# A gated attention, WKV and mixture-of-experts stack: late expert weights in raw buffers of their own, and the hand-written order of work behind the last attention tile

## The chip, the cores and the metric

The kernel runs on one core of one Trainium2 chip. Its time is the device time of one launch in microseconds; a median of several launches is given. Below, PE is TensorE, DVE is VectorE, ACT is ScalarE, POOL is GpSimd and SP is SyncE.

## What is computed

The input x has 16 batches of 64 tokens of 256 values. Four residual blocks follow one another, each on a LayerNorm of x and with a tanh gate:

```python
x = x + tanh(g_xattn[0]) * attention(layernorm(x), mask, ctx)      # 32 heads of 8, rope, additive mask, plus an adapter over ctx
x = x + tanh(g_ffn[0]) * moe0(layernorm(x))                        # 8 experts of 256x256, the best one, its softmax weight
x = x + tanh(g_xattn[1]) * wkv(w, u, layernorm(x), ctx)            # running max, exp, decayed sums over the 64 tokens
x = x + tanh(g_ffn[1]) * moe1(layernorm(x))                        # 8 experts, top 2, integer softmax; h = silu(x w1) * (x w3); h w2
```

The last block is the large one: 704 inner columns, and every token goes to two experts.

## The kernel before

**Tiles.** The 1024 tokens are eight tiles of 128 (two batches each). The function `tile` of every engine works on tile t for attention, on t-1 for the first experts (`experts0`, `mix`) and WKV's start, and on t-2 for WKV's output, the fourth LayerNorm (its result h4 goes to a table in HBM) and the router logits. Each engine's order of work is written by hand; engines meet through semaphores (`after` and `wait_ge`), and each engine and each DMA queue runs its list strictly in order.

**Slots.** The last block gathers tokens by expert in slots of 128 rows, each slot with one expert. There are NJ = 23. The first N1 = 5 (0 to 4, the early ones) are filled with the tokens of the first T1 = 6 tiles, as soon as these are routed, while tiles 6 and 7 are still in work; the other N2 = 18 (5 to 22, the late ones) need the routing of all tiles. Routing is `select` (top 2), `ranks` (a place for every token), `rows_of` (one-hot rows, L1236) and a matmul with them, `early_table` or `late_table` (L1690, L1717), whose result is the list of token numbers for the gathers. The softmax weights go through a chain of their own: `shares`, `looked_up`, `weigh`, `split` on DVE, then the matmul `early_weights` or `late_weights` (L1698, L1724).

**One slot.** POOL gathers 128 rows of h4 into `xg` (L529 to L537) and adds the result to the output by another indirect DMA (L549). SP loads the expert's up weights, 1.4 MB, into `w13[j % 2]` (L426). PE transposes the rows (`early_rows` L1742, `turn_rows` L1734), runs `up` in three column chunks, transposes h (`turn_h`, L1783) and runs `down` (L1794) with `w2`, of which all eight experts are loaded once (L445). ACT computes Silu (`gates`, L800) and copies out; DVE multiplies (`gates`, L1269). Early slots use the 32-bit weights as they are (L1758). Late slots split weights and rows into a high and a low part in another 32-bit format (F32R): ACT copies `wh` (`high_w`, L595), DVE subtracts `wl` (`low_w`, L1276), PE runs three matmuls for each (L1774). There `w13[j % 2]` is free once `wl` of slot j-2 is there:

```python
def late13(j, par):
    e = sp.value_load(ej[0:1, bass.ts(j - N1, 1)], min_val=0, max_val=NE - 1)
    after(sp, w_lo, j - 2 - N1, NC, NC)
    stream(j, par, e)
...
for j in (N1, N1 + 1):
    sp.wait_ge(up_mm, NC * (j - 1))
    late13(j, j % 2)
```

For slots 5 and 6 the buffer is that of slots 3 and 4, so SP waits for their `up` (L450).

**Behind the last tile.** Behind tile 7 PE runs, in a list written out by hand, the rest of tile 7 (output, experts0, WKV, router), the five early slots and the routing of the late ones; then come `slots(j, par)` in a loop. Four things in this stretch are touched. WKV's arguments: DVE scans (`wkv_args`, L1041), takes the difference dd (L1044) and clamps it eight times with a column added (L1047, L1048) into AR; ACT takes exponentials of AR (`decay`, L698, L700); DVE scans again (`wkv_scans`, L1056, L1060). ACT's order: an ACT_TABLE_LOAD stands in the trace at every switch between Exp and Silu. The w2 loads: SP issues them once the last `values` is done (L445). The order of `mix`, `weigh`, `split`, the gates and the weight tables on DVE.

## Time and profile before

| | |
|---|---|
| time, median of 3 runs | 566.99 us (565.34 to 567.60) |
| the profiled execution | 563.98 us; its span 562.1 us |
| busy: PE, DVE, ACT, POOL | 87%, 70%, 48%, 30% of the span |
| mean granted TensorE clock | 0.937 of 2.4 GHz |
| activation table loads behind tile 7 | 5 |
| late slots | 18, from 419.65 us on at 7.66 us each |

A row of the timeline or of the chain gives the start in us from the span's beginning and the duration. A bracket at the end of a row is the time that the engine stood idle before it, and what ended that wait. Matmuls are pipelined, so that durations of neighbours overlap.

### The profile page before, as it was taken

The numbers are of one execution on the slowest core, as the hardware profiler recorded it, in microseconds if no ns is written. First come the engines' busy times: TensorE is split into PE (matmuls) and PEld (weight loads), VectorE is DVE, ScalarE is ACT, GpSimd is POOL, SyncE is SP. The second block draws the span as 40 slices with busy tenths as digits, with TensorE's granted clock in tenths as the row PEclk, the third lists the DMA queues.
The fourth block names the chain that finished last, engine by engine and source line by source line (L and its number), as shares of the span: only waits on it lengthen the run. The fifth ranks groups of instructions, "written<-read, shape, count | busy, mean of one in ns | idle before, by whom it ended". The sixth has DMA issues, their size and how long they took to land. (4 is left out here: it accounts for less than half of the span.)

```text
span 562.1 us, 10467 instructions
## 1 busy us (share of the span) xinstructions
PE 486.9 (87%) x3147; PEld 361.2 (64%) x3148; DVE 395.0 (70%) x1040; ACT 267.0 (48%) x555; POOL 170.3 (30%) x228
## 2 busy tenths in 40 slices
PE   1585999899898999999996966798869999999994
PEld 0263767667576678577685753564558888788882
DVE  6454568788888887896886585896666666666640
ACT  1736356274373462651741225152446666666751
POOL 3070111314114113122131113322334556656622
PEclk9867999999999997997995886998999999999998
DMA  8800000000000000000000059434576776667821
GB/s 218 241 2 5 2 6 2 1 24 3 2 23 1 5 19 0 14 9 0 26 2 4 22 203 414 178 121 150 176 231 194 233 241 217 205 212 221 237 28 19
DMA packets 20944, 54.97 MB, mean 98 GB/s; under 512 B 5832, under 2 KB 15568, under 8 KB 17968
## 3 DMA queue, kind: packets, MB, share of 16 engines
q1 hardware_dynamic: 15632, 47.99, 24.9%
q0 software_dynamic: 4416, 6.03, 5.9%
q10 hardware_dynamic: 864, 0.54, 0.3%
q8 instruction: 17, 0.28, 0.2%
q14 instruction: 15, 0.12, 0.1%
HBM read 48.79 MB, written 5.24 MB: 96 GB/s over the span
## 5 line engine op out<-in xcount | busy, mean ns | idle before, releaser
L1794 PE MATMUL bank_o<-w,hT 128*128 (+1 forms) x276 | 68.0, 388 | 1.1 <-DVE hT L1262 0.7
L467 POOL TENSOR_SCALAR rstd<-mv 128x1 f32<-128x1 f32 x32 | 7.2, 226 | 185.6 <-DVE mv L904 185.6
L1276 DVE TENSOR_TENSOR wl<-up,wh 128x1024 fp32r<-128x1024 f32 (+1 forms) x54 | 60.9, 1128 | 0.7 <-ACT wh L595 0.7
L970 DVE TENSOR_REDUCE mx<-bank_s 128x8 f32<-128x512 f32 x64 | 43.5, 688 | 24.5 <-PE bank_s L1555 23.0
L1794 PEld LDWEIGHTS bank_o<-w,hT 128*128 128x128 f32 (+1 forms) x276 | 49.0, 189 | 15.2 <-issue 9.7
L595 ACT ACTIVATE wh<-up 128x1024 fp32r<-128x1024 f32 (+1 forms) x54 | 53.0, 982 | 4.5 <-DMA up<-in_w 4.5
L1553 PE MATMUL bank_s<-Kh,Qx 128*128 128x128 f32 x256 | 46.3, 309 | 5.9 <-ACT Qx L634 5.7
L1553 PEld LDWEIGHTS bank_s<-Kh,Qx 128*128 128x128 f32 x256 | 40.3, 218 | 8.8 <-issue 6.5
L634 ACT ACTIVATE Qx<-qs,CN 128x512 fp32r<-128x512 f32 x64 | 40.1, 709 | 5.2 <-DVE qs L949 5.2
L1269 DVE TENSOR_TENSOR hh<-sg,bank_s 128x256 f32<-128x256 f32 x46 | 19.2, 417 | 32.5 <-ACT sg L800 32.5
L549 POOL DMA_INDIRECT out_x<-ys,idx_out x18 | 29.0, 1609 | 37.4 <-ACT ys L811 36.6
L1602 PEld LDWEIGHTS bank_o<-Vx,Pt 128*64 128x64 f32 x1024 | 32.5, 138 | 8.1 <-issue 3.4
L1602 PE MATMUL bank_o<-Vx,Pt 128*64 128x18 f32 x1024 | 35.6, 212 | 0.5 <-ACT Oc L595 0.5
L657 ACT ACTIVATE Pt<-bank_t 128x512 f32<-128x512 f32 x48 | 27.9, 594 | 16.5 <-PE bank_t L1589 16.5
L1026 DVE SCALAR_TENSOR_TENSOR X<-bank_t,comb,X 128x256 f32<-128x256 f32 (+1 forms) x64 | 30.9, 482 | 6.7 <-PE bank_t L1646 4.8
L811 ACT ACTIVATE ys<-bank_o,tb 128x256 f32<-128x256 f32 x23 | 10.9, 474 | 43.7 <-PE bank_o L1794 38.7
L1262 DVE COPY hT<-bank_c 128x256 f32<-128x256 f32 x23 | 9.8, 425 | 27.4 <-PE bank_c L1783 27.3
L537 POOL DMA_INDIRECT xg<-normed,idx_in x17 | 24.5, 1442 | 13.9 <-POOL idx_in L534 13.9
L800 ACT ACTIVATE sg<-bank_s 128x256 f32<-128x256 f32 x46 | 17.7, 385 | 19.7 <-PE bank_s L1758 14.7
L534 POOL COPY idx_in<-gi 128x1 int32 (+1 forms) x17 | 25.9, 1521 | 0.0
L1646 PE MATMUL bank_t<-w0h,h2h 128*128 128x512 f32 x64 | 23.1, 443 | 2.8 <-DVE X L1026 1.7
L1583 PE MATMUL bank_t<-Qx,Kl 128*128 128x512 f32 x48 | 21.3, 443 | 4.6 <-ACT Pt L657 4.6
(328 smaller groups left out, 1177.9 us busy)
## 6 DMA issues: line engine op xcount, KB each, us to landing
up<-in_w SPq DMA_DIRECT2D x23, 1408.0 KB, 6.4
w<-in_w SPq DMA_DIRECT2D x4, 1536.0 KB, 16.0
CT<-in_ctxT SPq DMA_DIRECT2D x1, 1024.0 KB, 9.7
Pt<-in_WT SPq DMA_DIRECT2D x1, 1024.0 KB
mrow<-mhl SPq DMA_DIRECT2D x64, 8.0 KB, 1.9
X<-in_x SPq DMA_DIRECT2D x1, 896.0 KB, 7.0
out_x<-X SPq DMA_DIRECT2D x6, 128.0 KB, 1.7
normed<-h SPq DMA_DIRECT2D x6, 128.0 KB, 1.7
```

Of the source, the lines that this page charges most:

```text
L534: pool.tensor_copy(idx_in[par][:, :], gi[:, bass.ts(j - N1, 1)]).then_inc(idx_cp, 1)
L537: pool.indirect_dma_start(xg[par][:, :], None, H4, bass.IndirectOffsetOnAxis(ap=idx_in[par][:, :], axis=0)).then_inc(gathered[par], 16)
L549: pool.indirect_dma_start(rows, bass.IndirectOffsetOnAxis(ap=at_rows, axis=0), ys[par][:, :], None, compute_op=ALU.add).then_inc(added, 16)
L595: return act.activation(dst, src, ACT.Copy, scale=scale)
L634: act.activation(Qx[par][:, :, :, h, :], qs[:, :, :, :].bitcast(F32), ACT.Copy, scale=CN[:, C_HM + h:C_HM + h + 1]).then_inc(qx, 1)
L657: act.activation(Pt[:, g % 2, :, b, :], ((bc, ba)[b] if g == 0 else bt[b])[:, :].rearrange("p (h q) -> p h q", h=HG), ACT.Exp).then_inc(p_ ...
L970: dve.tensor_reduce(mx[:, b, :, g, :].rearrange("p s n -> p n s"), bs[n % 2][:, :].rearrange("p (n s k) -> p n s k", n=NP, s=2), AX.X, ALU ...
L1026: link(dve.scalar_tensor_tensor(X[:, u, :], bt[n % 2][:, j * HID:(j + 1) * HID], comb[:, e:e + 1], X[:, u, :], ALU.mult, ALU.add))
L1276: dve.tensor_tensor(wl[par][:, :, at:at + k], w13[par][:, :, at:at + k], wh[par][:, :, at:at + k].bitcast(F32), ALU.subtract).then_inc(w_l ...
L1553: pe.matmul(o[:, p * P:(p + 1) * P], Qx[par][:, g, b, 2 * p:2 * p + 2, :], Kh[par][:, b, g, :], start=(p == 0), stop=False)
L1602: ins = pe.matmul(bo[b * S:(b + 1) * S, h * VW:(h + 1) * VW], Pt[:, g % 2, h, b, :], Vx[par][:, g * HG + h, b, :, :].rearrange("p s d -> p ...
L1794: ins = pe.matmul(bo[:, 0:HID], hT[0:k, i, :], w2[0:k, bass.ts(e, 1), i, :].rearrange("p o n -> p (o n)"), start=(i == 0), stop=(i == IT - 1))
```

## The change

SP's late loads go into two new buffers `lw` with semaphores of their own, without the wait for `up_mm`; `high_w` and `low_w` read from there. The w2 loads wait for the first gather on either buffer. In the last tile the first two score groups stand ahead of `turn_comb` on PE, and the router of tile 5 ahead of `values` and `heads_out`. For tiles 6 and 7 the eight clamps are done by ACT as Relu (AR's first half negated, and the Exp then taken with scale -1). ACT does the softmax gate before the first Silu, and an Exp of one column stands before `evac_kk`. The early weights' table goes to bank_t, and `weigh`, `split` and its products change places. The rows of slots 3 and 4 go to bank_t instead of bank_o. `late_table` comes behind `turn_h(3)` and the first chunk of slot 4. The late weights' chain is spread over slots 5 and 6, on DVE and on PE. Indentation is cut in the diff.

```diff
@@ -154,6 +154,7 @@
 uc = sb("uc", [P, KT])
+nwc = sb("nwc", [P, KT])
 nuc = sb("nuc", [P, KT])
@@ -270,6 +271,9 @@
+lw = [keep(f"lw{i}", [P, KT, 2 * I]) for i in range(2)]
+scr = keep("scr", [P, 1])
+
 w2 = late("w2", [P, NE, IT, HID])
@@ -304,11 +308,13 @@
 ld_w2, ld_w13 = sem("ld_w2"), [sem(f"ld_w13{i}") for i in range(2)]
+ld_lw = [sem(f"ld_lw{i}") for i in range(2)]
 w_hi, w_lo, x_hi, x_lo = sem("w_hi"), sem("w_lo"), sem("x_hi"), sem("x_lo")
...
 route_step, rk_mm, tb_mm, route, e_of = sem("route_step"), sem("rk_mm"), sem("tb_mm"), sem("route"), sem("e_of")
+clamped = sem("clamped")
 nd_mul, nd_sum = sem("nd_mul"), sem("nd_sum")
@@ -422,32 +428,32 @@
-def stream(j, par, e):
-    sp.dma_start(w13[par][:, :, :].rearrange("p c n -> p (c n)"),
-                 w_rows[:, bass.ts(e, 1), 0:W13].rearrange("p o n -> p (o n)")).then_inc(ld_w13[par], 16)
+def weights(dst, e):
+    return sp.dma_start(dst[:, :, :].rearrange("p c n -> p (c n)"), w_rows[:, bass.ts(e, 1), 0:W13].rearrange("p o n -> p (o n)"))
...
     after(sp, up_mm, j - 2, NC, NC)
-    stream(j, j % 2, e)
+    weights(w13[j % 2], e).then_inc(ld_w13[j % 2], 16)
...
     after(sp, w_lo, j - 2 - N1, NC, NC)
-    stream(j, par, e)
+    weights(lw[par], e).then_inc(ld_lw[par], 16)
...
 sp.wait_ge(pv_mm, NT * G)
+for i in range(2):
+    sp.wait_ge(gathered[i], 16)
 for e in range(0, NE, 2):
...
 for j in (N1, N1 + 1):
-    sp.wait_ge(up_mm, NC * (j - 1))
     late13(j, j % 2)
@@ -693,9 +699,22 @@
-def decay(u):
-    after(act, arg_in, u, 1, 1)
-    act.activation(EX[:, :, :, :], AR[:, 0, :, :, :], ACT.Exp).then_inc(dec_exp, 1)
+def clamp(u):
+
+    after(act, wkv_step, u, 3, 2)
+    after(act, dec_exp, u - 1, 3, 3)
+    for c in range(KT):
+        for i, col, neg in ((0, wc, nwc), (1, nuc, uc)):
+            act.activation(AR[:, 0, i, c, :], dd[:, c, :], ACT.Relu, scale=-1.0, bias=neg[:, c:c + 1])
+            ins = act.activation(AR[:, 1, i, c, :], dd[:, c, :], ACT.Relu, bias=col[:, c:c + 1])
+    ins.then_inc(clamped, 1)
+
+def decay(u, sign=1.0):
+    if sign > 0:
+        after(act, arg_in, u, 1, 1)
+    else:
+        after(act, clamped, u - (NT - 2), 1, 1)
+    act.activation(EX[:, :, :, :], AR[:, 0, :, :, :], ACT.Exp, scale=sign).then_inc(dec_exp, 1)
     for i in range(2):
@@ -753,8 +772,10 @@
     attend(t, 1)
+    if prev2 and not nxt:
+        router(t - 2)
     heads_out(t, 0)
-    if prev2:
+    if prev2 and nxt:
         router(t - 2)
@@ -771,10 +792,10 @@
-def rows_in(j):
+def rows_in(j, o=bo, at=HID):
     after(act, xT_mm, j, 1, 1)
     after(act, up_mm, j - 1, NC, NC)
-    copy(xgT[:, :, :], bo[:, HID:HID + KT * P].rearrange("p (c n) -> p c n", c=KT)).then_inc(xT_in, 1)
+    copy(xgT[:, :, :], o[:, at:at + KT * P].rearrange("p (c n) -> p c n", c=KT)).then_inc(xT_in, 1)
@@ -783,10 +804,10 @@
     if n == 0:
-        after(act, ld_w13[par], j, 8, 16 - 8 * par)
+        after(act, ld_lw[par], j - N1, 8, 16 if par == N1 % 2 else 8)
         after(act, up_mm, j - 2, NC, NC)
     at, k = 2 * CHUNKS[n][0], 2 * CHUNKS[n][1]
-    copy(wh[par][:, :, at:at + k], w13[par][:, :, at:at + k]).then_inc(w_hi, 1)
+    copy(wh[par][:, :, at:at + k], lw[par][:, :, at:at + k]).then_inc(w_hi, 1)
@@ -812,30 +833,34 @@
 evac_ao(u, bt[1])
-decay(u - 1)
+clamp(u - 1)
 rows_in(0)
-gates(0, 0)
+decay(u - 1, -1.0)
 evac_h2(u)
...
 gate(u)
+gates(0, 0)
+evac_comb(u)
 gates(0, 1)
...
 rows_in(1)
-evac_comb(u)
 h_turned(0)
 gates(1, 0)
+act.activation(scr[:, :], tg[:, 0:1], ACT.Exp)
 evac_kk(u, bt[0])
+clamp(u)
+decay(u, -1.0)
+scaled(0, 0)
+rows_in(2)
 gates(1, 1)
 gates(1, 2)
-decay(u)
-scaled(0, 0)
-rows_in(2)
 h_turned(1)
...
 gates(2, 1)
+gates(2, 2)
+rows_in(3, bt[1], 0)
 scaled(1, 1)
 store_x(u - 1)
-gates(2, 2)
 store_h4(u - 1)
@@ -843,14 +868,13 @@
 router(u, bt[0])
+gates(3, 0)
 h_turned(2)
-rows_in(3)
-gates(3, 0)
 gates(3, 1)
 gates(3, 2)
+rows_in(4, bt[1], 0)
 scaled(2, 0)
 h_turned(3)
-rows_in(4)
 gates(4, 0)
@@ -858,10 +882,12 @@
 scaled(3, 1)
+h_turned(4)
 rows_high(N1)
...
 def slots(j, par):
-    h_turned(j - 1)
+    if not (isinstance(j, int) and j == N1):
+        h_turned(j - 1)
     high_w(j + 1, 1 - par, 0)
@@ -1034,14 +1060,18 @@
-def wkv_args(u):
+def wkv_args(u, clamps=True):
     link = Chain(dve, wkv_step, u, 3)
+    if not clamps and u == NT - 1:
+        dve.wait_ge(clamped, 1)
     after(dve, kk_in, u, 1, 1)
...
     link(dve.tensor_tensor(dd[:, :, :].rearrange("p c (b s) -> p (c b) s", b=BT), Op[:, :, 0:S], kk[:, :, :], ALU.subtract))
+    if not clamps:
+        return
     for c in range(KT):
@@ -1200,7 +1230,7 @@
     dve.wait_ge(tw1_mm, 1)
-    w3 = ba[:, 0:3 * N1].rearrange("p (k j) -> p k j", k=3)
+    w3 = bt[1][:, 0:3 * N1].rearrange("p (k j) -> p k j", k=3)
     step(dve.tensor_copy(tw1[:, :], w3[:, 0, :]))
@@ -1273,7 +1303,7 @@
     at, k = 2 * CHUNKS[n][0], 2 * CHUNKS[n][1]
-    dve.tensor_tensor(wl[par][:, :, at:at + k], w13[par][:, :, at:at + k], wh[par][:, :, at:at + k].bitcast(F32),
+    dve.tensor_tensor(wl[par][:, :, at:at + k], lw[par][:, :, at:at + k], wh[par][:, :, at:at + k].bitcast(F32),
                       ALU.subtract).then_inc(w_lo, 1)
@@ -1313,7 +1343,8 @@
 dve.tensor_scalar(nuc[:, :], uc[:, :], -1.0, None, ALU.mult).then_inc(prep, 1)
-dve.wait_ge(prep, 4)
+dve.tensor_scalar(nwc[:, :], wc[:, :], -1.0, None, ALU.mult).then_inc(prep, 1)
+dve.wait_ge(prep, 5)
@@ -1390,40 +1421,41 @@
 dve.wait_ge(zr, 2)
-wkv_args(w)
+wkv_args(w, False)
+shares(0, T1)
 residual1(u)
 ln_stats(1, u)
-shares(0, T1)
+looked_up(0, 3)
 ln_apply(1, u)
-looked_up(0, T1)
-gates(0, 0)
+looked_up(3, T1)
+weigh(0, T1)
 gate(u)
-gates(0, 1)
-gates(0, 2)
 wkv_scans(w)
 mix(u, 0)
-weigh(0, T1)
+gates(0, 0)
 mix(u, 1)
-split(0, T1)
-early_weights()
+gates(0, 1)
 mix(u, 2)
+gates(0, 2)
 mix(u, 3)
...
 ln_stats(2, u)
-early_weights_in()
+split(0, T1)
 h_turned(0)
 ln_apply(2, u)
+early_weights()
 gates(1, 0)
-wkv_args(u)
+wkv_args(u, False)
+wkv_inverse(w)
+wkv_out(w)
+early_weights_in()
+wkv_products(dve, u)
+wkv_scans(u)
 gates(1, 1)
 gates(1, 2)
-wkv_inverse(w)
-wkv_out(w)
-wkv_products(dve, u)
-wkv_scans(u)
-h_turned(1)
 wkv_sums(dve, u)
 gates(2, 0)
+h_turned(1)
 wkv_inverse(u)
@@ -1450,28 +1482,33 @@
 low_w(N1, N1 % 2, 2)
+h_turned(4)
 rows_low(N1)
-h_turned(4)
-shares(T1, NT)
-looked_up(T1, NT)
-weigh(T1, NT)
-split(T1, NT)
-late_weights()
...
         h_turned(j - 1)
+    if isinstance(j, int) and j == N1 + 1:
+        split(T1, NT)
+        late_weights()
     gates(j, 0)
     low_w(j + 1, 1 - par, 0)
+    if isinstance(j, int) and j == N1:
+        shares(T1, NT)
+        looked_up(T1, NT)
     gates(j, 1)
...
     low_w(j + 1, 1 - par, 2)
+    if isinstance(j, int) and j == N1:
+        weigh(T1, NT)
...
 slots(N1, 1)
+slots(N1 + 1, 0)
 late_weights_in()
-with dve.Fori(N1 + 1, NJ - 1, 2) as j:
+slots(N1 + 2, 1)
+with dve.Fori(N1 + 3, NJ - 1, 2) as j:
     slots(j, 0)
@@ -1561,32 +1598,41 @@
+def scores(t, par, g, b, prev, nxt):
+
+    if g == 0:
+        after(pe, k_lo, t, BT, BT)
+        if nxt:
+            after(pe, v_in, t + 1, 4, 2 * b + 2)
+            after(pe, k_in, t + 1, BT, b + 1)
+        else:
+            after(pe, (aoT_in, x1_in)[b], t - 1, 1, 1)
...
+    o = (bc, ba)[b] if g == 0 else bt[b]
+    q = Qx[par][:, g, b, :, :]
+    pe.matmul(o[:, :], Kl[par][:, b, g, :], q, start=True, stop=False)
+    pe.matmul(o[:, :], Kh[par][:, b, g, :], q, start=False, stop=False)
+    pe.matmul(o[:, :], mk2[par][:, b, :], Idup[:, 0:S].rearrange("p (o q) -> p o q", o=1).to_broadcast([P, HG, S]),
+              start=False, stop=False)
+
+def shift(t, par, g, b):
+    o = (bc, ba)[b] if g == 0 else bt[b]
+    if g == 0:
+        after(pe, m_row, t, BT * 64, BT * 64)
+    pe.matmul(o[:, :], Lm[:, :], mrow[:, b, g * 512:(g + 1) * 512], start=False, stop=True).then_inc(t_mm, 1)
+
 def attend(t, par, g, prev, nxt):
...
     for b in range(BT):
...
+        if nxt or g > 0:
+            scores(t, par, g, b, prev, nxt)
+        shift(t, par, g, b)
@@ -1695,7 +1741,7 @@
     for i in range(TOPK * T1):
-        ins = pe.matmul(ba[:, 0:3 * N1], ohp[:, i, :], valw1[:, i, :, :].rearrange("p k j -> p (k j)"),
+        ins = pe.matmul(bt[1][:, 0:3 * N1], ohp[:, i, :], valw1[:, i, :, :].rearrange("p k j -> p (k j)"),
                         start=(i == 0), stop=(i == TOPK * T1 - 1))
@@ -1734,12 +1780,13 @@
-def early_rows(j):
+def early_rows(j, o=bo, at=HID):
     after(pe, gathered[j % 2], j, 8, 16 - 8 * (j % 2))
     after(pe, xT_in, j - 1, 1, 1)
-    after(pe, y_sc, j - 2, 1, 1)
+    if o is bo:
+        after(pe, y_sc, j - 2, 1, 1)
     for c in range(KT):
-        ins = pe.transpose(bo[:, HID + c * P:HID + (c + 1) * P], xg[j % 2][:, c * P:(c + 1) * P], ident)
+        ins = pe.transpose(o[:, at + c * P:at + (c + 1) * P], xg[j % 2][:, c * P:(c + 1) * P], ident)
     ins.then_inc(xT_mm, 1)
@@ -1835,6 +1882,9 @@
         turn_q(t + 1)
+    if not nxt:
+        for b in range(BT):
+            scores(t, par, 0, b, prev, nxt)
     if prev:
@@ -1849,8 +1899,10 @@
     attend(t, par, 1, prev, nxt)
+    if prev2 and not nxt:
+        router_logits(t - 2)
     values(t, par, 0, prev)
-    if prev2:
+    if prev2 and nxt:
         router_logits(t - 2)
@@ -1896,62 +1948,70 @@
 turn_h(0)
+early_up(1, 0)
+early_up(1, 1)
+turn_h3(u, False, bt[0])
+early_up(1, 2)
 early_weights()
-early_up(1, 0)
-turn_h3(u, False, bt[0])
-early_up(1, 1)
-pe.wait_ge(wts1_in, 1)
-early_up(1, 2)
 pe.wait_ge(e1_of, 1)
...
 early_down(0, e)
+pe.wait_ge(wts1_in, 1)
 turn_y(u - 1, bt[1])
 early_rows(2)
+early_up(2, 0)
 turn_h(1)
-early_up(2, 0)
 early_up(2, 1)
+early_up(2, 2)
+turn_y(u, bt[0])
+pe.wait_ge(x3_in, u)
+early_rows(3, bt[1], 0)
 e = early_expert(1)
 early_down(1, e)
-turn_y(u, bt[0])
-early_up(2, 2)
+after(pe, xT_in, 3, 1, 1)
 turn_h4(u - 1, (u - 1) % 2, bt[1])
+early_up(3, 0)
 router_logits(u - 1, bt[1])
+after(pe, x3_in, u, 1, 1)
 turn_h4(u, u % 2, bt[0])
+turn_h(2)
 router_logits(u, bt[0])
-turn_h(2)
-early_rows(3)
-early_up(3, 0)
+early_up(3, 1)
 late_ranks()
-early_up(3, 1)
 early_up(3, 2)
+pe.wait_ge(rl_in, u)
+early_rows(4, bt[1], 0)
 e = early_expert(2)
 early_down(2, e)
+turn_h(3)
+early_up(4, 0)
 late_table()
-turn_h(3)
-early_rows(4)
-for n in range(NC):
-    early_up(4, n)
+early_up(4, 1)
+early_up(4, 2)
 e = early_expert(3)
 early_down(3, e)
+turn_h(4)
+pe.wait_ge(route, 1)
 turn_rows(N1, N1 % 2)
-turn_h(4)
 up(N1, N1 % 2)
-late_weights()
 turn_rows(N1 + 1, (N1 + 1) % 2)
...
 down(4, e)
-pe.wait_ge(wts_in, 1)
 pe.wait_ge(e_of, 1)
...
     up(j, par)
+    if isinstance(j, int) and j == N1 + 1:
+        late_weights()
     turn_rows(j + 1, 1 - par)
...
-with pe.Fori(N1 + 1, NJ - 1, 2) as j:
+slots(N1 + 1, 0)
+slots(N1 + 2, 1)
+with pe.Fori(N1 + 3, NJ - 1, 2) as j:
     slots(j, 0)
...
```

## Rows read from the trace of the kernel before

**Rows 1.** Windows: stretch, its us, each engine's busy us (instructions), granted clock, DMA share, GB/s.
```profile
335.00:341.81 6.81, 2.73 (x7) 1.50 (x7) 5.36 (x23) 1.62 (x4) 3.84 (x6) 0.50 1.00 418
...
407.06:419.65 12.59, 8.22 (x50) 6.09 (x49) 9.81 (x32) 4.85 (x9) 2.98 (x4) 1.00 0.71 231
...
419.65:427.31 7.66, 7.66 (x39) 6.21 (x39) 4.91 (x8) 4.60 (x8) 2.95 (x4) 1.00 0.59 202
```

**Rows 2.** Chain of waits (start, us, what): one `up` of a late slot, 12 matmuls.
```profile
420.50 2.81 PE bank_s L1774 x12
```

**Rows 3.** Timeline, PE (start, us, line, operation, idle before): early slots, before late ones.
```profile
335.25 0.66 PE L1490 MATMUL bank_t<-CN,ao 128*128 128x128 f32 x2 [2.76 <-DVE ao L993]
...
341.81 0.66 PE L1742 MATMUL bank_o<-CN,xg 128*128 128x128 f32 x2 [3.36 <-DMA xg<-normed,gi]
...
343.14 3.75 PE L1758 MATMUL bank_s<-up,xgT 128*128 128x512 f32 x4 [0.68 <-ACT xgT L595]
...
372.21 3.68 PE L1758 MATMUL bank_s<-up,xgT 128*128 128x512 f32 x8
...
385.51 3.52 PE L1758 MATMUL bank_s<-up,xgT 128*128 128x512 f32 x4 [0.52 <-ACT xgT L595]
...
412.46 0.60 PE L1724 MATMUL bank_t<-valw,ohp 128*128 128x54 bf16 x16 [1.27 <-DVE valw L1249]
...
419.65 0.63 PE L1783 MATMUL bank_b<-CN,hh 128*128 128x128 f32 x4 [1.89 <-issue]
```

**Rows 4.** Timeline, PE: the last tile, turn_comb.
```profile
307.84 0.38 PE L1631 MATMUL bank_t<-CN,comb 128*8 128x128 f32 x1 [1.91 <-DVE comb L1016]
```

**Rows 5.** Timeline, DVE: the first routing of select begins.
```profile
323.17 0.19 DVE L1097 TENSOR_SCALAR li<-LG 128x48 int32<-128x48 f32 x1 [1.44 <-ACT LG L595]
```

**Rows 6.** Timeline, SP: issues of the first up loads and of w2.
```profile
328.88 1.49 SPq L426 DMA_DIRECT2D up<-in_w  x2
...
332.04 2.01 SPq L445 DMA_DIRECT2D w<-in_w  x4
```

**Rows 7.** Timeline, POOL: issue of the first gather.
```profile
335.05 1.22 POOL L529 DMA_INDIRECT xg<-normed,gi  x1 [14.20 <-issue]
```

**Rows 8.** Landing of the gathers (tile xg, 325 to 430).
```profile
DMA to landing us min/median/max: 2.8/5.8/9.9
```

**Rows 9.** Landing of the four w2 loads (tile w).
```profile
DMA to landing us min/median/max: 11.0/16.0/21.4
```

**Rows 10.** Timeline, DVE: weights of the early table, between the mixes.
```profile
354.81 0.37 DVE L1179 TENSOR_SCALAR small<-small 128x6 f32<-128x6 f32 x1
...
356.50 0.15 DVE L1183 TENSOR_TENSOR wts<-small 128x6 f32<-128x6 f32 x1
...
357.72 0.17 DVE L1188 CAST wp<-wts 128x12 bf16<-128x12 f32 x1
...
358.76 0.69 DVE L1198 TENSOR_TENSOR valw<-val,wp 128x30 bf16<-128x30 bf16 x6
```

**Rows 11.** Timeline, DVE: the first and last of the eight clamps of tile 7.
```profile
366.63 0.29 DVE L1047 TENSOR_SCALAR AR<-dd,wc 128x128 f32<-128x128 f32 x1
...
368.01 0.28 DVE L1048 TENSOR_SCALAR AR<-dd,nuc 128x128 f32<-128x128 f32 x1
```

**Rows 12.** Timeline, DVE: select, ranks and rows_of of the late table.
```profile
384.38 0.18 DVE L1097 TENSOR_SCALAR li<-LG 128x16 int32<-128x16 f32 x1 [1.68 <-ACT LG L595]
...
389.18 0.23 DVE L1213 TENSOR_TENSOR gtj<-bank_t,CN 128x64 f32<-128x64 f32 x1 [1.85 <-PE bank_t L1709]
...
393.68 2.49 DVE L1236 TENSOR_TENSOR ohp<-posb,pos 128x512 bf16<-128x512 bf16 x4
```

**Rows 13.** Page part 5: ACT with a per-partition scale operand.
```profile
L634 ACT ACTIVATE Qx<-qs,CN 128x512 fp32r<-128x512 f32 x64 | 40.1, 709 | 5.2 <-DVE qs L949 5.2
```

**Rows 14.** Timeline, ACT: one table load of five, and the first high_w of slot 6.
```profile
368.24 1.28 ACT L698 ACT_TABLE_LOAD   x1
...
412.18 1.06 ACT L595 ACTIVATE wh<-up 128x1024 fp32r<-128x1024 f32 x1 [4.53 <-DMA up<-in_w]
```

28 lines of the change are left out of this document (6 added, 22 removed).

## The prediction, made before the change was run

> **What bounds the kernel now.** The windows come first. From 419.65 us on, one late slot takes 7.66 us and TensorE is busy for all of it at full clock [rows 1]; 17 such slots and a tail of 12 us follow, and no edit shortens them. The eight attention tiles before about 300 us are touched by one instruction only. So the change has to pay, or cost, between 300 and 420 us: all that counts is how much earlier turn_h(5) starts, which is at 419.65 today. In that stretch TensorE is not full. In 335.00 to 341.81 it is busy for 2.73 of 6.81 us, at 0.50 of its clock, with the DMA engines full at 418 GB/s; in 407.06 to 419.65 for 8.22 of 12.59 [rows 1]. The timeline of PE says why. It stood 2.76 us for the heads and came back at the lower of its two levels (1.2 GHz), stood 3.36 us for the first gathered rows, and ran its first `up` chunk of 4 matmuls in 3.75 us where 8 take 3.68 at full clock; the first chunk of slot 3 was slow again, 3.52 us for 4 [rows 3]. ACT stood 4.53 us for the weights of slot 6, until 412.18 [rows 14], and turn_h(5) then waited behind the chain that this began. Between the two lies a chain of small steps: mix, LayerNorm, WKV, router, select, ranks, table.
>
> **The change part by part.** All times are of the profiled execution. "Earlier" is counted at the same point of the program.
>
> Last tile. Six score matmuls move into the 1.91 us that PE waits for `comb` [rows 4]. One costs 2.81/12 = 0.23 us at full clock [rows 2], so 0.47 at half: 2.8 us there, 0.9 more than the wait. They save 1.4 us later, and PE is busy 2 us sooner, which should return its clock sooner by as much (up to 1.0 us). Between 0.5 and 1.5; I take 1.0. The router moves ahead of 32 `values` matmuls and a heads_out, so that select no longer stands 1.44 us for LG [rows 5]. Sum: select, the early table and the gathers behind them **2.4 earlier**.
>
> First gather. It is issued at 335.05 - 2.4 = 332.65 [rows 7], the two up loads at 328.88 - 2.4 = 326.5, the second 1 us later [rows 6]. 2.9 MB at 418 GB/s [rows 1] are 6.9 us: they are in by about 335.4. The w2 loads, issued at 332.04 today and so sharing the engines with the gather, come behind both gathers. Gathers land 2.8 to 9.9 us from issue, median 5.8 [rows 8]; without w2 beside it I take 4.1, so 336.8, against 341.8 today, and bounds of 335.4 (PE is free at 336.0) and 342. With 1.2 us for the transposes and their copy out, the first `up` starts at 338.0 instead of 343.14: **2.7 more**, most of the 3.36 us wait. I leave it at half clock, since it follows a stand of the same 2.8 us. SP now waits for both gathers; queued behind it are the four w2 issues (2.01 us [rows 6]), early13(2) to (4) and all late loads. Nobody wants early13(2) before 364, so only w2 can hurt: it starts at about 338 and lands, by the median and the longest of today [rows 9], at 354 to 360. Its first user, down(0), comes at 359: covered, with nothing to spare at the longest.
>
> From the first `up` to h3. Out of the DVE chain between the mixes go weigh, 354.81 to 356.65, split and the products, 357.72 to 359.36 [rows 10], and the 0.5 us of early_weights_in: 4.0 us. The early weights' table moves to bank_t and behind up(1,2), where PE has room. In come three gates products of some 0.35 each, which stood ahead of the chain before; half of split hides behind the rstd of POOL, its other half shows at 0.1. **2.8 earlier.** The gate's Exp ahead of Silu and the Exp of `scr` take two of five table loads away (1.28 us each, and the Exp after one starts at once [rows 14]); one lay mostly beside DVE's work and the other beside PE's, so 0.3 is in the 2.8.
>
> The trace has no Relu on ACT. Eight clamps take DVE 366.63 to 368.29, 1.66 us [rows 11]. The nearest ACT row with a per-partition operand takes 709 ns for 512 columns [rows 13]. Taking off 384 columns at about 0.85 ns and the overlap of 0.09 leaves 0.30 for one of 128, 2.4 us for eight; bounds are 1.7 and 5.0 (eight at the whole row's spacing of 0.62). For tile 6 it hides behind the gather; for tile 7 it is on the chain. I take 2.4, **0.8 later**. The Trainium skill, page "ScalarE: Activation LUTs", section "Rules for kernel authors", says relu, max and min belong on VectorE; by its price of 280 ns plus 0.83 per column less 93 of overlap, eight are 2.35 us as an estimate, and it speaks against this edit as the row does.
>
> From h3 to the second select. Besides the clamps: gates(1,1) now waits for the Silu load that comes after decay (0.6), turn_h4(7) stands behind up(3,0) on PE (0.9), and early_rows(2) on bank_o waits for y_sc(0), which comes after decay now (0.3; slots 3 and 4 go to bank_t and wait for the residual and the router instead, both done by then). With the 0.8, **2.6 later**; bounds 1.5 and 5.
>
> From the second select to up(5): 384.38 to 407.06 today, 22.7 us [rows 1, 12]. After the change DVE needs 2.5 for select, 0.3 for h_turned, 4.2 for ranks and 2.4 for rows_of [rows 12], with 0.3 and 0.6 of gates and waits of 0.3 between: 10.6 us until h of slot 3 is whole. PE has up(3,1), the ranks, up(3,2), rows and down(2) meanwhile, 7.3 us, and must stand 3.3 for turn_h(3), because the table now comes behind turn_h(3) and up(4,0). Then turn_h(3) 0.75, up(4) 4.75 (3.68 for its eight wide matmuls alone [rows 3] is a bit more than they take in a row), the table 0.6, down(3) 2.85, turn_h(4) 0.75, turn_rows 0.3 and rows_high 0.8: 10.8. Together 21.4, **1.3 earlier**: the table itself is 1.7 later, but up(4,0) is behind us and DVE's `tables` stands for nobody. e_of comes at 383, and the weights of slots 5 and 6 go into buffers of their own at once; two more loads of 6.9 us together have landed by 394, before high_w asks.
>
> That is at full clock. A stand of 2.76 us brought the half clock today [rows 3]; the nearest row says that it comes here too, over turn_h(3), up(4,0) and the table: **2.2 later**. Below that, zero: the 1.89 us of stand at 419.65 did not bring it (the slot after it runs at 1.00) [rows 1, 3].
>
> From up(5) to turn_h(5): 12.59 us now [rows 1]. Without the stand on the slot 6 weights it is a slot less its turn_h, 7.66 - 0.8, plus 0.3 for rows_high: 7.2, **5.4 earlier**. DVE's shares and looked_up (1.3 us) between its gates fit: its chain ends about 0.7 before PE asks.
>
> Late weights. Their 16 matmuls (0.60 us [rows 3]) lay in the stall; in slot 6 they lie on a full PE: **0.6 later**. DVE's split and products, 2.2 us, delay low_w(7) to some 0.2 before PE wants it. The one instruction for nwc costs 0.2 at the start, beside others.
>
> Sum: -2.4 - 2.7 - 2.8 + 2.6 - 1.3 + 2.2 - 5.4 + 0.6 = -9.2 us. The profiled execution took 563.98 us, so 554.8 for its like; the median of the three runs is 3.0 higher, 566.99, and from it **557.8**.
>
> **The rivals.** (1) The half clock does not come at turn_h(3): the late slots start 2.2 sooner, 555.6. For it: PE stands 3.3 us but was dense before; against: 2.76 sufficed. (2) The front's gain is given back: a gather or the DVE chain is late by 4 to 5 us, and only the slot 6 term stays, -5.4 + 0.6: 562.2. For it: DVE is one long chain in this stretch; against: its waits are few. (3) Relu needs a table of its own: two loads round the clamps of tile 7, 2 x 1.28 [rows 14] = 2.6, so 560.4. Copy never loads one in this trace, Relu isn't in it. The Trainium skill, same page, section "Table sets: the hidden batching unit", has relu in every set, which would rule this out; no row here shows it. (4) Slower: w2 behind the gathers. The place is down(0), at 359. w2's last piece lands up to 21.4 after the issue [rows 9], the issue follows the second gather's landing. It costs 1 us per us once that landing passes 338, and undoes all of the 9.2 once it passes 347; if it lands 20 us after its issue, at 354, w2 is in at 376 and the time is 557.8 + 17 = 575. Against: the longest gather took 9.9 [rows 8]. (5) The change does not do what it says: the loads of slots 5 and 6 are still late by another wait on SP, and the front's gain is lost too: 567.
>
> **How the numbers follow.** The forecast 0.55, (1) 0.17, (2) 0.16, (3) 0.04, (4) 0.04, (5) 0.04. A measurement here can tell about 0.5%, 2.8 us. Faster: the forecast and (1) to (3), less 0.02 for the poor end of (2): 0.90. Same: (5) and that 0.02: 0.06. Slower: (4), 0.04. The range goes from 553.5, which is (1) with the clock back before the first `up` (1.9), to 562.5, which is (2), or the forecast with the gather at its upper bound (+5).
>
> **What would show it.** Right: the first `up` near 338; h3 of tile 7 near 356; eight Relu rows of 0.3 to 0.4 us; three table loads after 333; no wait of ACT for `lw`; a PE stand of about 3 us before turn_h(3), slow matmuls behind it; turn_h(5) near 410. Wrong: w2 named as what ended a PE wait; loads at the Relu rows; a late slot longer than 7.7 us.

## The result, and the profile after

The changed kernel took 560.7 us (median of four runs, 554.4 to 563.2) where the kernel before took 567.0 beside it: a ratio of 0.986, 95% interval 0.982 to 0.990. Run again beside others (r_after, below) it gave 0.990 (0.986 to 0.993). The forecast was 557.8 in a range of 553.5 to 562.5. All ratios here leave out executions that were over 1.5% longer than the fastest of the same kernel; the medians do not.

The profiled execution took 559.51 us. Its total is not to be laid straight against the 563.98 of before: the seven tiles ahead of the last one, whose code is the same but for one instruction, brought the last tile 2 us later (turn_heads of the last tile at 299.21 us, before 297.22). So all that follows is counted from that row to turn_h(6), the start of the steady late slots. From there to the end of the span it is 134.9 us here (557.5 - 422.59) and 134.8 before (562.1 - 427.31).

The windows of the changed kernel, cut at the first `up` (339.44), h3 of tile 7 (the LayerNorm result ahead of WKV, 357.19), the second select (381.73), up(5) (405.28), turn_h(5) (414.42) and turn_h(6), in the columns of [rows 1]:

```profile
299.21:339.44 40.23, 33.62 (x248) 25.70 (x249) 28.23 (x97) 11.88 (x33) 5.50 (x10) 0.75 0.23 87
339.44:357.19 17.75, 17.27 (x59) 10.21 (x60) 13.24 (x53) 5.66 (x16) 8.56 (x13) 0.90 1.00 396
357.19:381.73 24.54, 20.78 (x94) 12.24 (x93) 15.80 (x52) 11.78 (x30) 5.91 (x7) 1.00 0.58 189
381.73:405.28 23.55, 18.68 (x81) 11.21 (x79) 15.78 (x52) 7.79 (x17) 4.13 (x5) 0.86 0.45 149
405.28:414.42 9.14, 7.53 (x32) 5.57 (x32) 6.75 (x20) 4.05 (x7) 3.74 (x3) 1.00 0.58 190
414.42:422.59 8.17, 8.17 (x55) 6.59 (x55) 7.03 (x17) 5.18 (x9) 4.44 (x4) 1.00 0.64 202
```

| stretch | before | after | moved | forecast |
|---|---|---|---|---|
| last tile to first `up` | 45.92 | 40.23 | -5.7 | -5.1 |
| to h3 of tile 7 | 20.80 | 17.75 | -3.05 | -2.8 |
| to the second select | 20.44 | 24.54 | +4.1 | +2.6 |
| to up(5) | 22.68 | 23.55 | +0.9 | +0.9 |
| to turn_h(5) | 12.59 | 9.14 | -3.45 | -5.4 |
| to turn_h(6) | 7.66 | 8.17 | +0.5 | +0.6 |
| sum | 130.09 | 123.38 | -6.7 | -9.2 |

The 2.5 us that are missing lie in two rows, 1.5 in the third and 2.0 in the fifth; the other rows came about 1 us better than forecast. TensorE's timeline, the rows that answer to [rows 3]:

```profile
338.11 0.66 PE L1789 MATMUL bank_o<-CN,xg 128*128 128x128 f32 x2 [0.56 <-DMA xg<-normed,gi]
339.44 3.73 PE L1805 MATMUL bank_s<-up,xgT 128*128 128x512 f32 x4 [0.68 <-ACT xgT L601]
...
392.23 1.11 PE L1830 MATMUL bank_b<-CN,hh 128*128 128x128 f32 x4 [3.35 <-DVE hh L1299]
...
393.56 3.62 PE L1805 MATMUL bank_s<-up,xgT 128*128 128x512 f32 x4
...
410.43 0.44 PE L1780 MATMUL bank_t<-CN,xg 128*128 128x128 f32 x2 [1.03 <-DMA xg<-normed,idx_in]
411.44 3.05 PE L1841 MATMUL bank_o<-w,hT 128*128 x12 [0.58 <-issue]
```

The wait of 3.36 us for the first gathered rows is 0.56. The stand before turn_h(3) is 3.35 us, forecast at 3.3, and what follows it is at half clock (1.2 GHz), as forecast: up(4,0) takes 3.62 for four matmuls. The wait for the landing of slot 6's rows is 1.03 us, with down(4) queued behind it. The kernel before has it too, 0.79 us, behind the late weights' matmuls, so it was there to be seen:

```profile
413.86 0.44 PE L1734 MATMUL bank_t<-CN,xg 128*128 128x128 f32 x2 [0.79 <-DMA xg<-normed,idx_in]
```

Those rows are long on their way. The chain of waits has their transfer, and SyncE's timeline the load of slot 7's weights (1.4 MB), which starts 0.44 us after it, as soon as `low_w` of slot 5 has freed the buffer:

```profile
403.13 7.26 DMA xg<-normed,idx_in
```
```profile
403.57 0.34 SPq L432 DMA_DIRECT2D lw<-in_w  x1
```

ScalarE, from the clamps of tile 7 to the second router:

```profile
360.47 0.40 ACT L708 ACTIVATE AR<-dd,nwc 128x128 f32<-128x128 f32 x1 [1.44 <-DVE dd L1072]
...
362.52 0.39 ACT L709 ACTIVATE AR<-dd,nuc 128x128 f32<-128x128 f32 x1
...
365.54 1.28 ACT L821 ACT_TABLE_LOAD   x1
...
379.87 0.44 ACTq L732 DMA_DIRECT2D normed<-h  x1
380.36 0.38 ACT L601 ACTIVATE h4T<-bank_t 128x256 f32<-128x256 f32 x1 [0.71 <-PE bank_t L1527]
381.44 0.18 ACT L601 ACTIVATE LG<-bank_t 128x8 f32<-128x8 f32 x1 [0.70 <-PE bank_t L1719]
```

And VectorE, beside the same clamps and at the select:

```profile
360.47 1.75 DVE L1096 RECIPROCAL ND<-ND 128x256 f32<-128x256 f32 x1
...
364.22 0.76 DVE L351 TENSOR_TENSOR VE<-VE,CT 128x256 f32<-128x256 f32 x2 [1.07 <-ACT VE L719]
...
381.73 0.17 DVE L1127 TENSOR_SCALAR li<-LG 128x16 int32<-128x16 f32 x1 [3.90 <-ACT LG L601]
```

Eight Relus start 0.29 us apart, 2.44 us in all, and load no table; there are three loads after 333 us (before: five). They begin in the same moment as VectorE's reciprocal of tile 6. The select stands 3.90 us for the logits where it stood 1.68 [rows 12].

GpSimd, the late gathers (5) and (6), with the add of slot 2 between them:

```profile
399.12 1.02 POOL L538 DMA_INDIRECT xg<-normed,gi  x1 [19.14 <-DVE si L1275]
400.45 1.60 POOL L555 DMA_INDIRECT out_x<-ys,gi  x1 [0.30 <-issue]
...
403.13 1.16 POOL L543 DMA_INDIRECT xg<-normed,idx_in  x1 [0.82 <-POOL idx_in L540]
```

### The profile page after: what moved, and what is told of

Read it like the earlier page. It is cut to its first block and busy times, and to the rows that moved or that the text cites. A ratio compares the mean times of both kernels' runs of the same rounds, so it can differ in the third digit from the quotient of the medians.

```text
span 557.5 us, 10446 instructions
## 1 busy us (share of the span) xinstructions
PE 490.0 (88%) x3147; PEld 362.9 (65%) x3148; DVE 389.6 (70%) x1025; ACT 268.6 (48%) x570; POOL 170.2 (31%) x228
## 5 line engine op out<-in xcount | busy, mean ns | idle before, releaser
L1306 DVE TENSOR_TENSOR wl<-lw,wh 128x1024 fp32r<-128x1024 f32 (+1 forms) x54 | 60.9, 1128 | 0.2 <-ACT wh L601 0.2
L601 ACT ACTIVATE wh<-lw 128x1024 fp32r<-128x1024 f32 (+1 forms) x54 | 52.9, 980 | 0.0
L1821 PE MATMUL bank_s<-wh,xh 128*128 128x512 f32 x72 | 24.2, 417 | 0.5 <-ACT xh L601 0.5
L1592 PE MATMUL bank_s<-mk,Idup 128*128 128x256 f32 x64 | 24.3, 379 | 0.0
```

The lines of the kernel that those rows point to most:

```text
L601: return act.activation(dst, src, ACT.Copy, scale=scale)
L1306: dve.tensor_tensor(wl[par][:, :, at:at + k], lw[par][:, :, at:at + k], wh[par][:, :, at:at + k].bitcast(F32), ALU.subtract).then_inc(w_lo, 1)
L1821: ins = pe.matmul(o, x[:, c, :], w[:, c, cols], start=(i == 0 and c == 0), stop=(i == 2 and c == KT - 1))
```

## The experiments

Each variant was timed beside the kernel before. "To first up", "up(5) to turn_h(5)" and "to turn_h(6)" are read from its profile, the first and the last from turn_heads of the last tile.

| run | to first up | up(5) to turn_h(5) | to turn_h(6) | ratio (95%) |
|---|---|---|---|---|
| before | 45.92 | 12.59 | 130.09 | 1 |
| after | 40.23 | 9.14 | 123.38 | 0.986 (0.982-0.990) |
| r_after | 40.26 | 9.27 | 123.44 | 0.990 (0.986-0.993) |
| u1_w2_first | 42.99 | 9.20 | 126.51 | 0.988 (0.984-0.993) |
| u2_up_wait | 40.18 | 13.31 | 127.48 | 0.986 (0.981-0.991) |
| u4_both_back | 42.81 | 9.78 | 127.13 | 0.992 (0.989-0.996) |
| u3_dve_clamps | 40.15 | 9.05 | 123.81 | 0.986 (0.981-0.991) |
| p1_lw_alone | 44.67 | 11.38 | 129.06 | 0.998 (0.994-1.002) |
| p2_lw_and_weights | 44.69 | 7.07 | 125.33 | 0.993 (0.991-0.996) |
| v1_table_first | 40.33 | 7.06 | 118.75 | 0.978 (0.970-0.986) |
| v2_fill_stand | 40.22 | 9.04 | 118.40 | 0.979 (0.974-0.983) |
| v3_h4_first | 40.08 | 9.17 | 123.51 | 0.990 (0.987-0.993) |
| v4_both | 38.44 | 9.08 | 117.84 | 0.983 (0.978-0.988) |
| v5_gather_first | 40.20 | 7.10 | 117.62 | 0.975 (0.971-0.979) |

**How far the profiles can be trusted: r_after.** The changed kernel once more.

> The changed kernel itself, once more, beside the others of this call. Both theories: the stretches from the last tile's start agree with the first profile within 0.3 us (first up 40.2, turn_h(5) 115.2 after turn_heads of the last tile), and what differs between executions lies before that start.

As expected: 40.26 and, to turn_h(5), 115.27 (115.21 in the first profile). Yet its last tile began at 302.25 us, not 299.21. The windows of the same stretch, first of after, then of r_after, go with it; the column behind the five engines is the mean granted clock. The third row is a piece of r_after's stretch:

```profile
80.00:200.00 120.00, 110.29 (x865) 81.16 (x863) 100.95 (x278) 62.31 (x143) 26.12 (x53) 1.00 0.03 8
```
```profile
80.00:200.00 120.00, 113.08 (x850) 83.80 (x848) 97.79 (x268) 58.87 (x136) 25.84 (x52) 0.93 0.03 8
...
104.00:108.00 4.00, 4.00 (x19) 2.60 (x18) 3.79 (x13) 0.38 (x1) 0.38 (x2) 0.50 0.00 0
```

So 0.93 is no level of its own: it is the mean of full clock and of some pieces at half. Over the profiles of the changed kernel and its variants the last tile began between 296.29 and 303.73 us, and the runs of one kernel lie 3.4 to 11.5 us apart. A step of 1 to 4 us can be read from the trace, counted from the last tile; whether the medians show it is another question, and below both are given.

**The w2 loads: u1_w2_first.**

```diff
-            for i in range(2):
-                sp.wait_ge(gathered[i], 16)
             for e in range(0, NE, 2):
                 sp.dma_start(w2[:, e:e + 2, :, :] ...
```

> The changed kernel, but the w2 loads no longer wait for the first two gathers. Theory (as forecast, term of the first gather): the four w2 loads stand ahead of the gather on the DMA engines again, the gather takes about 5.8 us to land instead of 2.8, so the first up starts about 3 us later against the last tile's start (43 us instead of 40.2) and the end about 2 to 3 us later than the changed kernel. Rival: what follows (the kk of tile 7, the wait of the second table) swallows it, the first up moves by 3 us but the end by under 1 us. Second rival: the gather lands as before, nothing moves, and the gain of the front came from the order on TensorE alone.

The first `up` starts after 42.99 us, 2.8 later, and this 2.8 is still there at turn_h(6) (+3.1). Its timeline of TensorE has the old wait again:

```profile
338.45 0.66 PE L1787 MATMUL bank_o<-CN,xg 128*128 128x128 f32 x2 [3.42 <-DMA xg<-normed,gi]
```

The profile bears the theory out: 2.8 us at the first `up` where about 3 were expected. The medians show nothing: 560.3 against 560.7 and 561.4 for the changed kernel. A ratio here is good to 0.4 to 0.5%, some 2.5 us, and a difference of two of them to about 3 us, so they neither show nor rule out a loss of 3. The profiled execution's last tile happened to begin at 296.80.

**The wait for `up` ahead of the late loads: u2_up_wait.**

```diff
             for j in (N1, N1 + 1):
+                sp.wait_ge(up_mm, NC * (j - 1))
                 late13(j, j % 2)
```

> The changed kernel, but the loads of w13 for slots 5 and 6 wait for the up matmuls of slots 4 and 5 again, into the new raw buffers. Theory (term of up(5) to turn_h(5)): the load of slot 6 starts only after up(5) has ended, so the high and low parts of slot 6 come late again; the copy of the weights on ScalarE waits again some 4.5 us and the end is 3.5 to 5 us later than the changed kernel. Rival: loads from the gather's time on share the DMA queues with the gathers, so taking the early load away lets gather(6) land sooner, and the loss is only 1 to 2 us.

turn_h(5) is 4.1 us later, the expected number, but not for the expected reason. ScalarE does stand 3.28 us for `lw`. TensorE's timeline, though, names the gather:

```profile
410.88 0.69 PE L1781 MATMUL bank_t<-CN,xg 128*128 128x128 f32 x2 [2.60 <-DMA xg<-normed,idx_in]
412.13 5.41 PE L1842 MATMUL bank_o<-w,hT 128*128 x12 [0.56 <-issue]
417.47 0.66 PE L1831 MATMUL bank_b<-CN,hh 128*128 128x128 f32 x4
```

The rows of slot 6 landed 1.6 us later than in the changed kernel (a stand of 2.60, not 1.03), and down(4) behind the stand took 5.41 us instead of 3.05. Both together are 3.9, and the wait for the weights lies under them. The gather landed 8.8 us after its issue, 7.3 in the changed kernel; in this profile it did not land sooner, as the rival had it. Whether the landing was late because two loads now start around it (1.4 us ahead of its issue and 0.5 behind), or by chance, this run alone doesn't say. The ratio, 0.986, doesn't show the loss at all.

**Both transfers back: u4_both_back.** The two diffs together.

> The changed kernel with both transfers back as they were: w2 loads not waiting for the gathers, and the loads of slots 5 and 6 waiting for up(4) and up(5). Alone, the profiles of these two showed turn_h(5) 3.1 and 4.1 us later against the last tile's start, while the medians moved by under 1 us. Theory: the profiles are right and the medians were blurred by what the clock did in the first tiles, the two lie in different stretches and add up: turn_h(5) 7.2 us later than in the changed kernel (122.4 after the last tile's start), the time 5 to 8 us longer than that of the changed kernel of the same call. Rival: something later gives the loss back, and the median is less than 3 us longer.

Not additive: turn_h(5) is 3.6 us later and not 7.2, of which 2.6 are the w2 loads. The stretch from up(5) is 9.78 us with the wait for `up` in place:

```profile
410.10 0.44 PE L1779 MATMUL bank_t<-CN,xg 128*128 128x128 f32 x2 [0.65 <-DMA xg<-normed,idx_in]
411.12 3.05 PE L1840 MATMUL bank_o<-w,hT 128*128 x12 [0.58 <-issue]
415.11 0.66 PE L1829 MATMUL bank_b<-CN,hh 128*128 128x128 f32 x4 [0.95 <-DVE hh L1298]
```

The same late load, with ScalarE standing 3.83 us for it, and here it costs 0.6 us: the gather came 6.9 us after its issue and TensorE kept its clock. The two loads stand around it just as in u2 (1.4 us ahead and 0.5 behind), so why it landed in 6.9 here and in 8.8 there these two runs don't show. By this profile the early load is worth 0.6 in the changed kernel; the rest of u2's loss is a late gather and a clock that fell behind it. The ratio, 0.992 (0.989 to 0.996), is 1.4 us longer than r_after's 0.990, give or take 3: the 5 to 8 us of the theory are ruled out, and neither the 3.7 of the profiles nor nothing at all is. Something later that gives it back, as the rival had it, is not to be seen: from turn_h(6) to the end of the span it is 134.6 to 135.0 us in every profile.

**The late weights: p1_lw_alone, p2_lw_and_weights.** The first puts only the raw buffers, without the wait for `up`, into the kernel before. The second also moves VectorE's chain of the late weights and TensorE's 16 matmuls:

```diff
 h_turned(4)
-shares(T1, NT)
-looked_up(T1, NT)
-weigh(T1, NT)
-split(T1, NT)
-late_weights()
 ...
 # slots: shares and looked_up behind low_w(6, 0); weigh at the end of slot 5;
 # split and late_weights ahead of the gates of slot 6; TensorE's behind up(6)
```

> The kernel before, with only the two raw buffers for the late weights and without the wait for up ahead of their loads; all else as before. Theory (term up(5) to turn_h(5), forecast 5.4 us, 3.5 us seen in the whole change): the stretch from up(5) to turn_h(5) gets 4.5 to 5.4 us shorter here, since nothing else was moved that could take its place, so the time is 4.5 to 5.4 us less than before, half and more of the whole change. Rival: the stretch is bound below by the landing of the gather for slot 6 (issued with slot 5's), and gets only 3 to 3.5 us shorter, as in the whole change.

Missed by both theories: up(5) to turn_h(5) takes 11.38 us, 1.2 less than before, and the time is that of before (0.998). ScalarE no longer stands for the weights. VectorE, first of this run, then TensorE:

```profile
411.88 0.16 DVE L1168 TENSOR_SCALAR sc<-sc 128x16 f32<-128x16 f32 x1
...
415.38 1.20 DVE L1252 TENSOR_TENSOR valw<-val,wp 128x288 bf16<-128x288 bf16 x3
416.49 0.41 DVE L1272 TENSOR_TENSOR hh<-sg,bank_s 128x256 f32<-128x256 f32 x1
```
```profile
416.63 0.60 PE L1727 MATMUL bank_t<-valw,ohp 128*128 128x54 bf16 x16 [1.28 <-DVE valw L1252]
...
422.60 0.63 PE L1786 MATMUL bank_b<-CN,hh 128*128 128x128 f32 x4 [1.87 <-issue]
```

Shares to products are 4.6 us in one piece, and the gates of slot 5 start only at 416.49, 5.3 us after up(5) began. In the kernel before the same chain ended at 412.4, by VectorE's row there:

```profile
411.20 1.20 DVE L1249 TENSOR_TENSOR valw<-val,wp 128x288 bf16<-128x288 bf16 x3
```

The weights' copy began at 412.18 [rows 14]: two waits side by side, and the forecast had named one.

p1's profile has two more differences to that of before, which its edit doesn't explain. It reaches the first `up` 1.25 us ahead, and it loses 1.7 us in the first two chunks of up(4): 5.39 us for eight matmuls, in part at half clock, where before took 3.70 behind the same small stands (none over 0.53 us). p2's profile has both as well.

> The kernel before with the raw buffers for the late weights, without the wait for up, and also with VectorE's shares, looked_up, weigh, split and the products of the late weights, and TensorE's matmuls of them, moved into slots 5 and 6 as in the changed kernel. Theory, formed after the run with the buffers alone (up(5) to turn_h(5) 11.4 us instead of 12.6, gates of slot 5 starting only at 416.5 behind 4.6 us of the weights' chain on VectorE): with that chain out of the way too, the stretch is 7.5 to 9.2 us, the end 3.4 to 5 us earlier than before. Rival: what is left is the landing of the gather of slot 6, which TensorE needs ahead of down(4), and the stretch stays above 10 us.

7.07 us: with the chain out of the way the stretch is 5.5 shorter than before, the rival's floor of 10 is not there, and the whole is 3.7 us ahead of p1 at turn_h(6). The ratio, 0.993 (0.991 to 0.996), is clear of 1, where p1's was not. The other order, VectorE's chain moved and the load left late, was not run in the kernel before; u4, which has it in the changed kernel, took 9.78.

**The clamps: u3_dve_clamps.** `wkv_args(w)` and `wkv_args(u)` make the clamps on VectorE again, ScalarE's `clamp` calls go, and decay waits for `arg_in`.

> The changed kernel, but VectorE makes the clamps of tiles 6 and 7 again. Theory as forecast: the clamps cost the path 0.8 us more on ScalarE than on VectorE, so this variant is about 0.8 us faster than the changed kernel. Rival, from the trace of after: ScalarE's eight clamps lie beside VectorE's inverse of tile 6, so with the clamps back on VectorE the products of tile 7 come 0.5 to 1.5 us later, and so does the second table; the variant is 0.5 to 1.5 us slower. Second rival: both come out within 0.5 us, because the select of the second table waits for the evacuation of h4 and not for these.

h4 of tile 7 is turned 81.52 us after the last tile's turn_heads, 80.08 in the changed kernel: 1.4 later, the first rival. VectorE's clamps, 1.6 us, stand ahead of the reciprocal, which ScalarE's do not. Only 0.4 of the 1.4 is left at turn_h(6), and 0.9 of it was made up between the select and up(5): there TensorE came back from its 3.35 us stand at full clock here and dropped to half only at up(4,0):

```profile
393.45 0.66 PE L1828 MATMUL bank_b<-CN,hh 128*128 128x128 f32 x4 [3.35 <-DVE hh L1297]
...
394.32 3.42 PE L1803 MATMUL bank_s<-up,xgT 128*128 128x512 f32 x4
```

The times are the same within what can be told.

**The second select: v3_h4_first.**

```diff
             turn_h4(u - 1, (u - 1) % 2, bt[1])
-            early_up(3, 0)
             router_logits(u - 1, bt[1])
             ...
             router_logits(u, bt[0])
+            early_up(3, 0)
             early_up(3, 1)
```

and on ScalarE `store_x(u)`, `store_h4(u)` behind `router(u)`.

> The changed kernel, with turn_h4 and router of tiles 6 and 7 and turn_h(2) ahead of up(3,0) on TensorE, and on ScalarE the stores of tile 7 behind the evacuation of h4 and the router's. Theory (missed step, h4 to select takes 4.5 us instead of 2.3): the select of the second table comes 1.5 to 2 us earlier against h4 of tile 7, and the end 1 to 2 us earlier. Rival: TensorE stands longer ahead of turn_h4(7) since h4 comes only at 377.2, up(3) is late instead, half clock starts there, and the end comes 1 to 3 us later although the select is earlier.

Select comes 1.2 us earlier against the last tile (81.35 us behind it, 82.52 in the changed kernel) and nothing comes of it. up(3,0) and up(3,1) now run in one piece ahead of late_ranks, and in part at half clock, as the rival had it: 5.38 us for eight matmuls, where v1 takes 3.60 for eight of up(4). TensorE's timeline, and then VectorE, whose part of the ranks was ready 2.6 us earlier:

```profile
379.72 0.61 PE L1719 MATMUL bank_t<-wg,h4T 128*128 128x8 f32 x4 [1.00 <-ACT h4T L601]
...
381.54 5.38 PE L1805 MATMUL bank_s<-up,xgT 128*128 128x512 f32 x8
```
```profile
387.07 0.23 DVE L1243 TENSOR_TENSOR gtj<-bank_t,CN 128x64 f32<-128x64 f32 x1 [2.11 <-PE bank_t L1755]
```

**The stand before turn_h(3): v1_table_first, v2_fill_stand, v4_both.** In v1 the late table's matmuls go ahead of turn_h(3); in v2:

```diff
 # TensorE
-            turn_h(3)
             early_up(4, 0)
             late_table()
+            turn_h(3)
             early_up(4, 1)
 # VectorE
-            h_turned(3)
             tables()
+            h_turned(3)
```

> The changed kernel, with the late table's matmuls put ahead of turn_h(3) on TensorE and VectorE's evacuation of the table ahead of its h_turned(3). Theory (missed step: both late gathers are issued only after up(4,0) and the table): gathers 5 and 6 are issued 4 to 5 us earlier, up(5) no longer waits and the transposes of slot 6's rows no longer wait for their landing; the end comes 1.5 to 2.5 us earlier than the changed kernel. TensorE still falls to half clock at turn_h(3). Rival: the table only moves work ahead of turn_h(3), the stretch to up(5) is bound by gates and matmuls, and the end moves by under 0.5 us.

> The changed kernel, with up(4,0) and then the late table's matmuls ahead of turn_h(3), and VectorE's table ahead of h_turned(3). Theory (the half clock is worth 2.2 us): the stand of 3.35 us ahead of turn_h(3) is filled, TensorE keeps its full clock there, up(4) runs at about 1.85 us for each chunk instead of 3.6, and the end comes 3 to 4.5 us earlier than the changed kernel. Rival: the clock falls all the same (somewhere a stand of that length stays, since the gates and not the matmuls set the pace), and only the earlier gathers' 1 to 2 us are won.

v1 is 4.6 us ahead of the changed kernel at turn_h(6), v2 5.0, both by more than was expected. TensorE in v1, then in v2:

```profile
392.48 0.27 PE L1763 MATMUL bank_t<-val,ohp 128*128 128x54 bf16 x4 [1.04 <-DVE ohp L1266]
...
394.79 0.66 PE L1830 MATMUL bank_b<-CN,hh 128*128 128x128 f32 x4 [0.31 <-DVE hh L1299]
...
395.50 3.60 PE L1805 MATMUL bank_s<-up,xgT 128*128 128x512 f32 x8
```
```profile
389.39 1.96 PE L1805 MATMUL bank_s<-up,xgT 128*128 128x512 f32 x4 [0.44 <-DVE hh L1299]
391.18 0.81 PE L1763 MATMUL bank_t<-val,ohp 128*128 128x54 bf16 x16
392.30 0.66 PE L1830 MATMUL bank_b<-CN,hh 128*128 128x128 f32 x4 [0.31 <-DVE hh L1299]
...
405.73 0.44 PE L1780 MATMUL bank_t<-CN,xg 128*128 128x128 f32 x2 [1.07 <-DMA xg<-normed,idx_in]
```

v1 still waits 2.2 us in all, in five pieces of at most 1.04 between small matmuls, and keeps full clock, against its expectation; it has no wait for slot 6's rows, and up(5) to turn_h(5) is 7.06. v2 has no stand over 0.44 there, reaches up(5) 4.9 us earlier, and keeps the wait for slot 6's rows (9.04). The times agree: 0.978 (from three runs) and 0.979 against 0.986 and 0.990.

Why v2 keeps that wait though its gather is issued 4.9 us earlier against the last tile, and v1 doesn't, the traces of all runs together show. What differs is the next load of weights on SyncE:

| run | next load, after gather(6)'s issue | gather(6) lands after |
|---|---|---|
| after, r_after, u1, u3, v2, v3, v4 | 0.4 to 0.5 us | 7.3 to 7.4 us |
| v1_table_first | 2.2 us | 5.3 us |
| v5_gather_first (below) | 3.4 us | 3.7 us |
| p1, p2 | 4.5 us | 3.2, 3.4 us |
| u2, u4 | 0.5 us, and one 1.4 us ahead | 8.8, 6.9 us |
| before | 0.3 us, and one at 2.2 us | 9.9 us |

In the changed kernel and its variants that is slot 7's load, which waits for `low_w` of slot 5, and in v2 both come forward together with the gather. No run holds this load back alone, so that it slows the gather is read from how the runs line up, not from an edit of its own.

> The edits of the two variants before together: h4 of tile 7 turned first, and up(4,0) and the late table ahead of turn_h(3). Theory: they lie in different stretches and add up, 4.5 to 6 us faster than the changed kernel. Rival: the select that comes earlier meets up(3) not yet begun, TensorE stands ahead of turn_h4(7) and goes to half clock there, and the two together are worth less than the fill alone.

Of v4's lead over the changed kernel (5.5 us), 1.8 is in the stretch to the first `up`, which has the same code: TensorE got its full clock back sooner there (a mean of 0.82 over the stretch, in v2 0.75). From the first `up` to turn_h(6) it takes 79.4 us, v2 78.2: the edit of v3 costs 1.2 on top of v2. The rival's mechanism, then: the eight matmuls of up(3,0) and up(3,1) take 5.38 us here too, with late_ranks behind them. That the edit brings the half clock is read from these two profiles; p1 and p2 had such a fall at up(4) without it.

**A better kernel: v5_gather_first.** v2 with two more edits:

```diff
 # GpSimd
             gather(5, 1)
-            add(2, 0)
-            pool.wait_ge(route, 2)
             gather(6, 0)
+            pool.wait_ge(route, 2)
+            add(2, 0)
 # TensorE
             up(N1, N1 % 2)
-            turn_rows(N1 + 1, (N1 + 1) % 2)
             e = early_expert(4)
             down(4, e)
+            turn_rows(N1 + 1, (N1 + 1) % 2)
```

> The changed kernel with up(4,0) and the late table ahead of turn_h(3) (as in the best variant so far), and with two more edits: GpSimd issues the gather of slot 6 ahead of the add of slot 2, and TensorE does down(4) ahead of the transposes of slot 6's rows. Theory: the wait of 1.07 us for these rows' landing goes, and down(4) no longer stands behind it; up(5) to turn_h(5) is 7.3 to 8 us instead of 9.04, the end 1 to 1.7 us earlier than the variant without them. Rival: turn_h(5) waits for VectorE's gates of slot 5, which end at about 407.2 of that profile, 2.4 us before turn_h(5), and the transposes that now come after down(4) delay the high and low rows of slot 6, so up(6) waits and the gain is under 0.5 us.

```profile
403.32 2.95 PE L1841 MATMUL bank_o<-w,hT 128*128 x12
406.20 0.44 PE L1780 MATMUL bank_t<-CN,xg 128*128 128x128 f32 x2
...
412.22 0.61 PE L1770 MATMUL bank_t<-valw,ohp 128*128 128x54 bf16 x16 [0.97 <-DVE valw L1279]
```
```profile
407.09 0.43 DVE L1312 TENSOR_TENSOR xl<-bank_t,xh 128x256 fp32r<-128x256 f32 x1 [1.02 <-ACT xh L601]
```

up(5) to turn_h(5) is 7.10 us, 1.9 less than v2. One slot later 0.97 comes back as a wait for the products of the late weights: VectorE had stood 1.02 us for the rows of slot 6, whose transposes now come behind down(4), and its chain of the late weights is queued behind that. So 0.8 is left, less than the theory had and more than the rival, whose mechanism this is in part. The rows had landed by 398.0, before up(5) began at 399.37, so the second edit may not have been needed; it was not run apart. It is the fastest median seen, 552.45 us (0.975, 0.971 to 0.979), 1.6% below that of the changed kernel beside it; the 1.3 us to v2's median are within what the runs scatter.

## Why the forecast held, and where it was off

**Last tile and first gather** (-2.4, -2.7): right, at -5.7. The w2 order is worth 2.6 to 2.8 (u1, u4). The rest is 1.7 to 3.1, since the kernel before needs 44.67 to 45.92 for this stretch in three profiles; no run takes the orders of scores and router back alone. w2 itself landed at most 18.0 us after its issue, by 358, two before down(0): rival (4) had its place and not its price. (The 335.4 at which the up loads are in doesn't follow from its own figures, 326.5 + 1 + 6.9 = 334.4; nothing in the sum hangs on it.)

**First `up` to h3** (-2.8): right, -3.05. The terms as listed (4.0 less 1.05 and 0.1) make 2.85 without the 0.3 of the table loads that is said to be in it; no run takes this order back, so its parts stay unmeasured.

**h3 to the second select** (+2.6): came as +4.1, with one sign wrong. The step "Eight clamps ... I take 2.4, 0.8 later" took the duration rightly (2.44) and compared it with VectorE's 1.66 as if both stood in the same queue. On ScalarE they run beside the reciprocal of tile 6, and from the scans to the products it was 5.1 us, before 5.6: no loss. The Trainium skill, page "ScalarE: Activation LUTs", section "Rules for kernel authors", puts relu on VectorE; here, on the path of tile 7, following it made h4 1.4 us later (u3). The estimate of 2.35 us from that page's price agrees with the 2.44. Rival (3) fell with the Relu rows, which no table load parts from the Exp ahead of them or behind. On the other side "turn_h4(7) behind up(3,0), 0.9" was short: h4 to select went from 2.31 to 4.54 us, because behind up(3,0) came the router of tile 6 on TensorE and the two stores' issues on ScalarE. Of these 2.2 us, 1.6 are TensorE's: its transposes of h4 of tile 7 start 2.1 us after VectorE's h4, before 0.5. v3 gets 1.2 us of this back for the select and loses them again behind up(3) at half clock.

**Second select to up(5)** (-1.3 + 2.2): right as a sum, and the half clock came at turn_h(3) after a stand of 3.35. From turn_h(3) to up(4,1) it is 5.46 us; in v2 the same pieces take some 3.3 (1.79 from up(4,0) to the table, 0.8 and 0.72), so 2.2 was the price. Rival (1) needed this not to happen; v1 and v2 made it so, and it was worth more than the 2.2, for another reason in each: v2 also filled 2.6 us of the stand itself, v1 filled 1.1 of it and no longer waits for slot 6's rows. "Below that, zero" was not safe either: at the start of the last tile in the kernel before, a stand of 1.67 us was followed by half clock (last section).

**up(5) to turn_h(5)** (-5.4, came as -3.45): the size of the possible gain was right, the cause was one part of it, and the place where it was taken back was not seen. "Without the stand on the slot 6 weights it is a slot less its turn_h, 7.2" is what p2 measured (7.07). But taking away the stand on the weights alone gives 1.2 (p1); VectorE's chain of the late weights, which I priced only for whether it "fits" between the gates, stood beside it, and moving it as well gives the other 4.3. In the other order the shares are others: with the chain moved and the load late it is 9.78 (u4), 2.8 less than before, and the early load adds 0.6. That the forecast's 7.2 met p2's 7.07 is therefore luck in part: the 7.2 rests on a move of the chain that its reasoning doesn't count. And in the changed kernel 2.0 of it goes to the rows of slot 6: the forecast had noted that "the table itself is 1.7 later" and closed the account there, without following the table to gather(6), issued at 403.13, which then takes 7.26 us with slot 7's load 0.44 us behind it. [rows 8] had landings up to 9.9; the early slots' term used them, this one used none. v1, with the table ahead, gets 7.06.

**Late weights** (+0.6): +0.5. The sum: -6.7 seen, -9.2 forecast, +1.5 and +2.0 from the two steps named and about 1 back from the others. By the medians the gain is 6.3 us in the first measurement and 4.6 in the second; by the ratios it is 8.0 and 5.7. That the median came as near as 2.9 us to the forecast is not all merit: two misses of 3.5 us together were evened out in part by about 1 the other way, and the start of the last tile alone moved by more than that between executions. Rival (2), "the front gain given back", was not the case: -8.75 in front, and 4.1 given back, of which 2.6 was in the sum.

## What to carry to other kernels

An idle engine has one releaser in the profile, but a wait that ends at the same moment on another engine is only seen by asking when each of the consumer's inputs would have been ready; 412.18 and 412.4 stood side by side here. Removing the first alone gave 1.2 of the 5.5 us that both were worth together, and the median didn't show it. When a step is moved later, follow its result to the last DMA that hangs on it, with that DMA's landing time, the large transfers that start beside it and whatever is queued behind it. And a stand of TensorE can cost more than itself: in one piece of 3.35 us it cost another 2.2, and other work put in its place was the cheapest gain of this study.

## What was not expected of the hardware

Seven tiles of the same code took between 296.3 and 303.7 us until the last tile began, which is as much as the whole change is worth. It goes with the mean clock granted between 80 and 200 us: 296.3 to 299.3 us in the eight profiles that had 1.00, 300.7 to 301.3 in the three with 0.97, and 302.3 to 303.7 in the three with 0.93. It isn't all of it: before and after both had 1.00 and began 2.0 us apart. Nor is it a matter of stands only: the half clock of r_after in 104 to 108 us came with TensorE busy for all of the 4 us before it. Why one execution is granted it and another isn't, these runs don't show. That u1 and u4 lost 3 to 4 us in the profile and less than 2 in the median is no more than the medians' own uncertainty; u2's profile had a late landing and a clock that fell behind it, and nothing says how often that happens.

A stand of 3.35 us didn't bring the half clock at once each time: in u3 the turn_h(3) behind it ran at full speed (0.66 for four transposes, in the changed kernel 1.11) and the four matmuls of up(4,0) at half (3.42 us). In u2, 2.60 us sufficed, and it cost 2.4 us in the down(4) behind it. In the kernel before a shorter one did, at the start of the last tile; two such transposes take 0.38 us at full clock:

```profile
297.22 0.69 PE L1490 MATMUL bank_c<-CN,ao 128*128 128x128 f32 x2 [1.67 <-DVE ao L993]
```

Yet the 1.89 us of [rows 3] and stands of up to 1.04 us in a row of small matmuls in v1 did not bring it, while in v3 and v4 the clock fell at up(3) behind stands of no more than 1.00 us, and in p1 and p2 at up(4) behind 0.53. The length of the last stand alone doesn't tell, in these traces, whether the clock falls.
